# Fetching 39 of 880 gathers with single-row DMAs from SP and ScalarE instead of GpSimd

## The reference, cut to what matters

```
h = relu(layernorm(x))
t = h @ w_nbr                                    # a table of 6250 rows, 1 KB each
agg = segment_sum(edge_weight[:, None] * t[src], dst)
x = x + agg + h @ w_own + bias
```

## Time and profile before

| | us |
|---|---|
| median of 3 runs (lowest, highest) | 5891.65 (5889.07, 5894.68) |
| the profiled execution, its own time | 5890.26 |
| its span in the profile | 5888.5 |
| the pass of Layer 2 within the span | 3124 to 4230 |

### The profile page before, as it was taken

How to read it: one execution, slowest core, us unless ns; L and a number is a source line. 1 busy time by engine, 2 the same in 40 slices (tenths; PEclk the granted TensorE clock), 3 DMA queues, 4 the chain that set the end, 5 groups by cost and what they waited for, 6 DMA issues and landing times. The chain is left out here.

```text
span 5888.5 us, 74164 instructions
## 1 busy us (share of the span) xinstructions
PE 4310.0 (73%) x16431; PEld 2538.7 (43%) x16431; DVE 4021.3 (68%) x9597; ACT 2385.8 (41%) x6625; POOL 3603.9 (61%) x4186
## 2 busy tenths in 40 slices
PE   2789999999986665665667787777784666666688
PEld 1544444444465444444444443343342444444444
DVE  5689999999985555555565555555576677677653
ACT  2498888888863333333330000000022333333322
POOL 3465555555534777777756777777617777777300
PEclk9999999999998777777777667767696877877799
DMA  7453333333335555555523333333425555555331
GB/s 166 156 172 98 98 97 98 99 97 98 97 88 158 139 144 144 139 144 144 140 85 99 105 105 106 105 105 106 137 82 147 145 148 145 145 148 146 99 116 44
DMA packets 486723, 711.79 MB, mean 121 GB/s; under 512 B 215564, under 2 KB 325600, under 8 KB 486134
## 3 DMA queue, kind: packets, MB, share of 16 engines
q0 software_dynamic: 171200, 474.81, 29.1%
q1 hardware_dynamic: 308688, 225.69, 13.2%
q10 hardware_dynamic: 6416, 6.55, 0.3%
HBM read 626.28 MB, written 76.66 MB: 119 GB/s over the span
## 5 line engine op out<-in xcount | busy, mean ns | idle before, releaser
L273 POOL DMA_INDIRECT G<-table,srcI x1760 | 1672.6, 950 | 582.6 <-issue 502.7
L542 PE MATMUL pS<-G,one 128*128 128x260 f32 (+1 forms) x3520 | 1198.7, 479 | 190.2 <-issue 95.1
L1371 POOL DMA_INDIRECT G<-table,srcI x880 | 831.4, 945 | 594.9 <-ACT zt L1395 544.6
L1507 PE MATMUL pM<-zt,one 128*128 128x512 f32 x1760 | 944.0, 618 | 115.2 <-DVE zt L1453 73.8
L623 POOL DMA_INDIRECT G<-table,srcI x880 | 833.3, 947 | 282.1 <-issue 162.1
L475 ACT ACTIVATE acc<-pS x1760 | 691.2, 393 | 773.8 <-PE pS L542 519.4
L659 PE MATMUL pM<-G,one 128*128 128x256 f32 x1760 | 805.7, 564 | 240.6 <-issue 118.4
L1395 ACT ACTIVATE zt<-G,a4S 128x128 f32<-128x128 f32 x2640 | 856.2, 389 | 0.0
L542 PEld LDWEIGHTS pS<-G,one 128*128 128x128 f32 x3520 | 590.9, 211 | 261.0 <-issue 207.0
L659 PEld LDWEIGHTS pM<-G,one 128*128 128x128 f32 x1760 | 380.3, 260 | 651.1 <-DVE one L632 516.6
L639 DVE TENSOR_TENSOR acc<-acc,pM 128x256 f32 x880 | 370.3, 421 | 395.6 <-PE pM L659 391.3
(11 more groups left out here) (321 smaller groups left out, 5419.3 us busy)
## 6 DMA issues: line engine op xcount, KB each, us to landing
G<-table,srcI POOLq DMA_INDIRECT x3520, 2.8
relT<-step_rel SPq DMA_DIRECT2D x220, 256.0 KB
a10T<-step_a SPq DMA_DIRECT2D x660, 30.0 KB
far<-step_rec SPq DMA_DIRECT2D x224, 64.0 KB
table<-row SPq DMA_DIRECT2D x100, 128.0 KB, 1.7
acc<-zero SPq DMA_DIRECT2D x21, 512.0 KB, 4.8
step_a<-part SPq DMA_DIRECT2D x7, 960.0 KB, 3.9
table<-row SPq DMA_DIRECT2D x50, 132.0 KB, 1.7
```

Source lines behind the costliest of these rows:

```text
L273: pool.indirect_dma_start(G[:, par * C + j, 0:ROW], None, tab, bass.IndirectOffsetOnAxis(ap=srcI[:, k:k + 1], axis=0)).then_inc(s_g[par * ...
L542: nc.tensor.matmul(sum_of(of[j]), one[:, par * C + j, :], G[:, par * C + j, :], start=False, stop=True, skip_group_check=True).then_inc(s_ ...
L1371: pool.indirect_dma_start(G[:, k % GS, :], None, table[0], bass.IndirectOffsetOnAxis(ap=srcI[:, k:k + 1], axis=0)).then_inc(s_g[k % GS], 16)
L1507: nc.tensor.matmul(pM[k % 2][:, :], one[q % 2][:, s, :], z_of(q)[:, s, :, :], start=True, stop=True).then_inc(s_m, 1)
```

## The change

The setup writes one more array to DRAM, `src_rows`: the 128 source nodes of each step as a row. In the pass of Layer 2, steps 43, 87, ..., 879 (20 of them) are fetched by SP and steps 65, 109, ..., 857 (19 of them) by ScalarE. GpSimd skips these steps; it issues the other 841 gathers as before, and its condition on step k - 16 is unchanged.

For each of its steps a fetching engine loads the row of source nodes into a small SBUF buffer (one step ahead), waits until the scatter of its step before the last has finished (it has two buffers of 128 rows of its own), and then, eight times over, loads sixteen values into registers and issues sixteen DMAs of one row of 1 KB each, whose source address comes from the register. So there are 128 DMAs for each of these steps, each adding 16 to one semaphore; TensorE waits for all 2048 on it and multiplies with the fetching engine's buffer instead of `G`.

```diff
+    src_rows = dram("step_src", [KP, P], I32)
...
+                PACE = 44
+                by_row = {"sp": range(PACE - 1, K, PACE), "act": range(PACE + PACE // 2 - 1, K, PACE)}
+                GR = {w: [se.sb(f"G_{w}{j}", [P, D]) for j in range(2)] for w in by_row}
...
+                def fetch(eng, w):
+                    ks = by_row[w]
+                    def indices(i):
+                        if i < len(ks):
+                            eng.dma_start(idx[w][i % 2][:, :], src_rows[ks[i]:ks[i] + 1, :]).then_inc(s_idx[w][i % 2], 16)
+                    indices(0)
+                    for i, k in enumerate(ks):
+                        indices(i + 1)
+                        if i >= 2:
+                            eng.wait_ge(s_m, ks[i - 2] + 1)
+                        eng.wait_ge(s_idx[w][i % 2], 16 * (i // 2) + 16)
+                        for z in range(0, P, 16):
+                            _, values = nc.values_load_multi_w_load_instructions(
+                                idx[w][i % 2][0:1, z:z + 16], engines=[eng.engine], min_val=0, max_val=NP - 1, ...)
+                            for q, v in enumerate(values):
+                                eng.dma_start(GR[w][i % 2][z + q:z + q + 1, :], rows[ds(v, 1), :]).then_inc(s_row[w][i % 2], 16)
...
                     def _(pool):
                         for k in range(K):
+                            if any(k in t for t in turns.values()):
+                                continue
                             freed(pool, s_m, k - u + 1)
...
                     def _(sp):
                         sp.dma_start(w_sb[:, :, :], w_own.rearrange("(c p) n -> p c n", p=P)).then_inc(s_w, 16)
+                        fetch(sp, "sp")
+                    @block.scalar
+                    def _(act):
+                        fetch(act, "act")
...
                             pe.wait_ge(s_one, k + 1)
-                            gathered(pe, u, s_g, k, j)
+                            buf, landed, count = source(k)
+                            pe.wait_ge(landed, count)
...
                             sp.dma_start(rel_rows.rearrange("(b p) e -> p b e", p=P), relH[:, :, :]).then_inc(s_rec, 16)
+                            sp.dma_start(src_rows.rearrange("(b p) e -> p b e", p=P), gsrc[:, :, :]).then_inc(s_rec, 16)
```

More of the change, by code:

```diff
@@ L617, in edge_sum, with source @@
                 s_g = [se.sem(f"s_g{j}") for j in range(u)]
+                PACE = 44
+                by_row = {"sp": range(PACE - 1, K, PACE), "act": range(PACE + PACE // 2 - 1, K, PACE)}
+                GR = {w: [se.sb(f"G_{w}{j}", [P, D]) for j in range(2)] for w in by_row}
+                idx = {w: [se.sb(f"idx_{w}{j}", [1, P], I32) for j in range(2)] for w in by_row}
+                s_idx = {w: [se.sem(f"s_idx_{w}{j}") for j in range(2)] for w in by_row}
+                s_row = {w: [se.sem(f"s_row_{w}{j}") for j in range(2)] for w in by_row}
+                turns = {w: {k: i for i, k in enumerate(ks)} for w, ks in by_row.items()}
+                def fetch(eng, w):
[11 more added lines that the diff above has]
+                            _, values = nc.values_load_multi_w_load_instructions(
+                                idx[w][i % 2][0:1, z:z + 16], engines=[eng.engine], min_val=0, max_val=NP - 1,
+                                skip_runtime_bounds_check_because="sources are nodes")
+                            for q, v in enumerate(values):
+                                eng.dma_start(GR[w][i % 2][z + q:z + q + 1, :], rows[ds(v, 1), :]).then_inc(s_row[w][i % 2], 16)
+                def source(k):
+                    for w in by_row:
+                        if k in turns[w]:
+                            i = turns[w][k]
+                            return GR[w][i % 2], s_row[w][i % 2], 16 * P * (i // 2 + 1)
+                    return G[k % u], s_g[k % u], 16 * len([j for j in range(k % u, k + 1, u) if all(j not in t for t in turns.values())])
                 with nc.Block() as block:
@@ L656, in scatter @@
                             pe.wait_ge(s_one, k + 1)
-                            gathered(pe, u, s_g, k, j)
+                            buf, landed, count = source(k)
+                            pe.wait_ge(landed, count)
                             freed(pe, s_acc, added(k - R))
-                            nc.tensor.matmul(pM[j % R][:, :], one[j % R][:, :], G[j][:, :], start=True, stop=True).then_inc(s_m, 1)
+                            nc.tensor.matmul(pM[j % R][:, :], one[j % R][:, :], buf[:, :], start=True, stop=True).then_inc(s_m, 1)
                             n = own_at(k)
@@ L985, in _ @@
                                 sp.dma_start(rows[r:r + 1, :], row[0:1, :]).then_inc(s_rec, 16)
-                            sp.wait_ge(s_rec, 96)
+                            sp.wait_ge(s_rec, 112)
                             sp.wait_ge(s_w2, 64)
```

## The result

The changed kernel takes 6072.7 us (median of 4 runs, 6072.3 to 6074.6) against 5891.3 us before: 1.0308 times as long, 95% interval 1.029 to 1.0326. The profiled execution took 6074.6 us, its span is 6072.8 us. The forecast was 6012 us, slower, by SP's queue; the direction and the mechanism came out, and the loss is 181 us instead of 121.

What follows compares the result with a forecast made beforehand. GpSimd's gathers, 1.2517 us a step, were taken to bound the kernel; with fetches of 61.0 us SP's queue would take over and end the stage 121 us later: 5890.26 + 121 = 6011, plus 1 for the median, 6012 us; range 5930 to 6240.

Steps and rivals of the forecast that it cites:

- GpSimd sets the pass, 1.2517 us a step: Layer 2 pass: GpSimd's gathers run without a break, so each step taken away saves 1.2517 us, 48.8 us for 39.
- A fetch has to be under 52.6 us to stay hidden: Between two of SP's steps GpSimd has 42 gathers, 52.6 us; a longer fetch makes SP's queue the bound.
- A row costs 0.405 us: Fetching queue, per single-row DMA: 0.29 us for the issue and 0.115 for its address instruction, 51.8 us for 128.
- A load costs 1.10 us: Fetching queue: a register load of 16 values takes 1.10 us with its gap, 8.8 us for the eight of a fetch.
- Index load and waits 0.4 us a fetch: Fetching queue: the small load of the indices and the two waits add 0.4 us to each fetch.
- T: Time of one fetch on its queue, 61.0 us, from 51.8 for rows, 8.8 for register loads and 0.4 for the rest.
- SP ends last and ScalarE is covered below 62.8 us: End of the stage: SP's last rows land at 4348, ScalarE's part ends at 4315, later only if its fetch exceeds 62.8 us.
- TensorE waits about 8 us, 20 times: TensorE's wait for SP's rows: 61.0 - 52.6, about 8 us, at each of SP's 20 steps.
- Rival (a): Fetches stay hidden if issue and address take at most 0.34 us a row; pass 48.8 us shorter, 5843; chance 0.30.
- Rival (d): All single rows back up on one DMA engine, full at 0.13 us a row; about 6390 at 0.2 us; chance 0.03.
- The sequencer's 512 cycles: Skill's sequencer time per DMA on earlier generations, estimated at 0.43 us; a fetch would take 84 us, the kernel about 6470.

Runs made afterwards that it cites:

- e1: Changed kernel with only SP fetching its 20 steps, ScalarE's 19 given back to GpSimd: 6070.6 us, 1.0301 of the kernel before.
- e11: Changed kernel with every 48th instead of every 44th step fetched by each queue, 36 steps in all: 5960.8 us, 1.0106 of the kernel before.
- e5: Changed kernel with every 55th instead of every 44th step fetched by each queue, 31 steps in all: 5859.9 us, 0.9933 of the kernel before.
- e6: Changed kernel with every 54th step fetched by each queue, side by side, 32 steps in all: 5853.0 us, 0.9922 of the kernel before.
- e9: Changed kernel with constant row numbers and only SP fetching, 20 steps, ScalarE's 19 back to GpSimd: 5864.5 us, 0.9946 of the kernel before.
- e3: Changed kernel with constant row numbers on both queues, no register loads or address computation: 5888.1 us, 0.9994 of the kernel before.

## Why the prediction was right

- *GpSimd sets the pass, 1.2517 us a step.* Shown by the runs in which the fetches are hidden: 31, 32 and 20 steps taken away brought 36, 43 and 32 us, where 38.8, 40.1 and 25.0 were worked out; the medians of those chips scatter by several us.
- *A fetch has to be under 52.6 us to stay hidden, and the queue becomes the bound if it is not.* Shown by `e1`, `e11`, `e5` and `e6`. It is the step that carries the result.
- *A row costs 0.405 us.* Measured 0.419 over a whole fetch, 1.8 us more for its 128 rows. It is this near by compensation: the DMA took 0.225 and not 0.25, the address instruction 0.037 and not 0.074, and there is a MOVE of 0.029 with its gap that no row of before had shown.
- *A load costs 1.10 us.* Too small: SP's took 1.232 us, with the gap 1.27. Eight of them are 1.4 us more a fetch.
- *Index load and waits 0.4 us a fetch.* About right: 64.1 - 128 x 0.419 - 8 x 1.27 leaves 0.3 us. In all the term of the sum that was mis-sized is T, 64.1 and not 61.0 us; 20 x 3.1 = 62 us more turn the 121 into 183. By the profiles the pass grew by 177 us: its last rows landed within 1.1 us of the last issue instead of 2, and the next stage began 1.2 us after the last add instead of 4.6. The 7 us by which the pass began later were in no term; it is by luck that they about make up for these two, so that the spans differ by 184 us and the medians by 181.
- *SP ends last and ScalarE is covered below 62.8 us.* Right: ScalarE's took 61.6 (its 19 fetches ended 111 us before SP's), and TensorE never waited for them.
- *TensorE waits about 8 us, 20 times.* The count was right, the size was not. The 8 us are what GpSimd lacks; TensorE works off what is ready faster than it comes in and then stands 24.7 us.
- *Rival (a), hidden and 48.8 us faster if issue and address cost 0.34 us or less.* Its condition was not met, with 0.408 us from row to row. It would also not have been enough for two queues: without addresses and loads SP alone needs 0.30 us a row and is hidden (`e9`), but with both queues the kernel is only level (`e3`), by the limit that they share.
- *Rival (d), all single rows on one engine that backs up.* It had 0.03 and was priced from 0.056 us a row. In the changed kernel it plays no part, as the issues are too slow to fill anything (SP's period is 64.0 us without ScalarE and 64.1 with it), and the price was near: the packets of a row took 0.062 us there. By that price `e3` should not have backed up either, and it did, at one row per 0.217 us from two queues. So the mechanism that the rival names, single rows that back up behind one another, is real and would have taken the gain of any cheaper issue on both queues; the way in which (d) priced it, by the time of the packets alone, does not find it.
- The sequencer's 512 cycles, which the prediction weighed from the Trainium skill ("DMA: Bandwidth & Descriptors", section "Why a DMA increments its semaphore by 16 and not by 1") and estimated at 0.43 us, don't hold here: the trace has 0.225 us.

## What to carry to other kernels

Work that is handed from a full queue to an idle one is free only while its whole length in that queue, every issue, address, register load and gap of it, is under the time in which the next piece is due; divide the one by the other before setting how often, since just above that point the loss is that of the whole queue and not of one piece. At 64 us for 128 rows, every 44th step cost 181 us and every 54th brought 43. And a second limit can lie right behind the first: with cheaper issues on both queues (`e3`) the kernel only came back to the time of before, at the limit that single-row DMAs of the two queues share.

## What the runs showed of the hardware that was not expected

- Single-row DMAs of 1 KB from SP's and ScalarE's queues together reached one per 0.217 us beside gathers that use 36% of the DMA engines, whereas SP's queue alone issued one per 0.299 us without any backlog. The packets of a row took 0.12 us in the first case and 0.06 to 0.07 in the second. With 256 bytes a row a fetch took SP 48 to 54 us instead of 56, as long as its queue did not pause, and the kernel was 0.25% slower than the one before.
- A register load of 16 values took 1.23 us and one of 32 took 2.13 on SP; 1.30 and 2.24 on ScalarE.
- A DMA with a register as its address took 0.225 us of SP's queue, less than the 0.25 of one with a constant; it has an address instruction of 37 ns and a MOVE of 29 ns ahead of it, and a row takes 0.408 to 0.419 us in all.
